# Relative-position attention with a binarised MLP: feed-forward jobs, normalisation steps and VectorE evacuations moved to other steps of a written-out order

## What is computed

```python
xn = layernorm(x)
x  = x + attn(xn) + ffn(xn)
# attn, 16 heads of 8 features: a second layernorm with gain and bias, then
content = einsum('bihd,bjhd->bhij', q + u_bias, k)
pos     = relative_shift(einsum('bihd,jhd->bhij', q + v_bias, p))
attn    = softmax((content + pos) * scale) @ v ;  attn = attn @ Wo + bo
# ffn: h = [xn, -xn], then three layers with weights of +1 or -1, 512, 512 and 128 wide
h = relu(s0 * h @ w0) * 2 ;  h = relu(s1 * h @ w1) * 2 ;  h = s2 * h @ w2
```

## Time and profile before

| | |
|---|---|
| median of 3 runs | 1533.58 us (1532.46 to 1533.88) |
| the profiled execution's own time | 1533.58 us |
| its span | 1531.8 us |
| granted TensorE clock, mean | 0.987 |
| TensorE (matmul) busy | 1488.4 us, 97% |
| VectorE busy | 1337.4 us, 87% |
| ScalarE busy | 1238.8 us, 81% |
| GpSimd busy | 717.8 us, 47% |
| DRAM traffic | 550.4 MB, 359 GB/s |
| load of a batch's x, issue to landing | 9.1 us, median of 16 |

### The profile page before, as it was taken

One profiled execution on the slowest core, in us unless ns is written; L12 is line 12 of the kernel. 1 busy time (PEld: TensorE's weight loads), 2 busy tenths in 40 slices (PEclk: granted clock), 3 DMA queues, 4 the chain that ended last, 5 costly groups with the idle time before them and its releaser, 6 DMA issues.

```text
span 1531.8 us, 41221 instructions
## 1 busy us (share of the span) xinstructions
PE 1488.4 (97%) x16040; PEld 981.4 (64%) x16040; DVE 1337.4 (87%) x3483; ACT 1238.8 (81%) x1368; POOL 717.8 (47%) x725
## 2 busy tenths in 40 slices
PE   6899999999999999999999999999999999999997
PEld 2466666666666666666666666666666666666664
DVE  4698989889898998989889898998989889898985
ACT  5688889888888888879888888888889888888873
POOL 5655636354563635537354463635536354533300
PEclk8799999999999999999999999999999999999998
DMA  3999999999999999999999999999999999999991
GB/s 132 331 373 363 374 381 368 385 352 396 367 372 387 348 393 362 359 387 361 386 358 387 367 367 393 352 388 367 377 383 360 388 363 386 362 384 368 369 412 65
DMA packets 80435, 550.40 MB, mean 359 GB/s; under 512 B 9329, under 2 KB 10097, under 8 KB 14705
## 3 DMA queue, kind: packets, MB, share of 16 engines
q1 hardware_dynamic: 42944, 278.35, 48.7%
q10 hardware_dynamic: 37296, 269.41, 46.9%
HBM read 274.57 MB, written 273.15 MB: 358 GB/s over the span
## 4 chain that ended last, share of the span: by engine, by line
PE 76%; DVE 13%; ACT 4%; DMA 3%; issue 3%; ACTq 0%; POOL 0%; DVEq 0%
PE ps_pt L694 27%; PE ps_av L708 13%; PE ps_job L635 12%; PE ps_pos L675 11%; DVE sc_sb L571 6%; DVE sc_sb L579 5%; PE ps_job L596 3%; PE ps_job L599 3%; DMA sc_sb<-shift 2%; PE ps_con L685 2%; ACT pt_sb L457 2%; PE ps_job L605 1%; ACT z_t L413 1%; PE ps_job L610 1%; PE ps_job L614 1%
## 5 line engine op out<-in xcount | busy, mean ns | idle before, releaser
L571 DVE CUSTOM_DVE_ANT_0 sc_sb<-ps_con,sc_sb 128x512 f32<-128x512 f32 x1024 | 664.2, 684 | 151.8 <-PE ps_con L685 143.8
L447 ACT COPY pos_sb<-ps_pos 128x1024 f32<-128x1024 f32 x510 | 519.0, 1018 | 139.8 <-PE ps_pos L675 135.3
L579 DVE TENSOR_SCALAR sc_sb<-sc_sb,nmax 128x512 f32<-128x512 f32 x1024 | 602.8, 620 | 0.1
L457 ACT ACTIVATE pt_sb<-ps_pt 128x1024 f32<-128x1024 f32 x512 | 524.8, 1025 | 59.0 <-PE ps_pt L694 57.0
L694 PE MATMUL ps_pt<-c_sb,sc_sb 128*128 128x128 f32 x4096 | 558.9, 280 | 7.9 <-ACT pt_sb L457 5.4
L694 PEld LDWEIGHTS ps_pt<-c_sb,sc_sb 128*128 128x128 f32 x4096 | 438.5, 141 | 134.9 <-issue 90.8
L708 PE MATMUL ps_av<-pt_sb,v_sb 128*9 128x128 f32 x8192 | 320.0, 274 | 1.3 <-issue 0.7
L685 PE MATMUL ps_con<-k_stack,q_stack 26*128 26x512 f32 x1024 | 301.3, 496 | 7.0 <-DVE nmax L571 1.9
L708 PEld LDWEIGHTS ps_av<-pt_sb,v_sb 128*9 128x9 f32 x8192 | 173.0, 90 | 196.5 <-issue 191.5
L675 PE MATMUL ps_pos<-p_stack,q_stack 26*128 26x512 f32 x1024 | 266.2, 500 | 6.7 <-ACT pos_sb L447 4.5
L351 POOL CAST h<-act_sb 128x512 fp32r<-128x512 f32 x128 | 78.6, 614 | 405.7 <-ACT act_sb L423 405.0
(11 more groups left out here) (88 smaller groups left out, 939.8 us busy)
## 6 DMA issues: line engine op xcount, KB each, us to landing
shift<-pos_sb SPq DMA_DIRECT2D x256, 1026.0 KB, 9.4
sc_sb<-shift ACTq DMA_DIRECT2D x256, 1024.0 KB, 10.6
x_sb<-in_x SPq DMA_DIRECT2D x16, 256.0 KB, 9.1
out<-x_sb SPq DMA_DIRECT2D x16, 256.0 KB, 11.2
stack_w_sb<-in_stack_w SPq DMA_DIRECT2D x1, 512.0 KB, 5.3
c_sb<-in_consts ACTq DMA_DIRECT2D x1, 422.0 KB, 3.3
o_t<-in_wp ACTq DMA_DIRECT2D x1, 256.0 KB, 5.9
heads<-in_pe_t ACTq DMA_DIRECT2D x1, 256.0 KB, 6.9
```

The lines of the kernel that those rows point to most:

```text
L447: act.copy(to, ps_pos[:, :, :]).then_inc(s_pe, 1)
L457: act.activation(pt_sb[:, 2 * i:2 * i + 2, :], ps_pt[:, :, :], ACT.Exp, scale=-1.0) \
L571: dve.tensor_tensor_reduce(sc_sb[:, m % N_SC, t, :], ps_con[:, k, :], sc_sb[:, m % N_SC, t, :], -SCALE, 3.4e38, ALU.add, ALU.min, nmax[:, ...
L579: dve.tensor_scalar(sc_sb[:, m % N_SC, t, :], sc_sb[:, m % N_SC, t, :], nmax[:, m % N_SC, t:t + 1], None, ALU.subtract).then_inc(s_sub, 1)
```

## The change

Three things move. (1) The tables: `L1 1` from half 6 to 5, `L0 0`, `L0 1` and `L0 2` of the next batch from halves 13, 14 and 19 to 18, 19 and 21, and `L0 3` from 32 (half 0 of the next batch) to 29. (2) `slot_of`: the statistics from slot 8 to 6 (half 16 to 12), `scales` and the first `norm` from slot 9 to 7 (half 18 to 14), the second `norm` from slot 11 to 10 (half 22 to 20). (3) On VectorE the copy of `ps_av` moves from the start of the half after to the end of the half itself, ahead of that half's jobs and statistics, and the jobs move from between the two subtractions to behind both and behind the copy.

```diff
         FIRST_NEXT = (... 
-                      (25, "V", 0), (27, "KG", 0), (32, "L0", 3))
+                      (25, "V", 0), (27, "KG", 0), (29, "L0", 3))
-        THIS = ((1, "QG", 1), (2, "L1", 0), (3, "KG", 1), (6, "L1", 1), (7, "QG", 2), (8, "L1", 2), (9, "KG", 2),
+        THIS = ((1, "QG", 1), (2, "L1", 0), (3, "KG", 1), (5, "L1", 1), (7, "QG", 2), (8, "L1", 2), (9, "KG", 2),
                 (10, "L1", 3), (15, "QG", 3), (16, "KG", 3), (28, "TO", 0), (30, "L2", 0, 2))
-        NEXT = ((11, "T1", 0), (13, "L0", 0), (14, "L0", 1), (17, "TZ", 0), (19, "L0", 2), (23, "QG", 0),
-                (25, "V", 0), (27, "KG", 0), (32, "L0", 3))
+        NEXT = ((11, "T1", 0), (17, "TZ", 0), (18, "L0", 0), (19, "L0", 1), (21, "L0", 2), (23, "QG", 0),
+                (25, "V", 0), (27, "KG", 0), (29, "L0", 3))
...
-            return [b if 0 <= b < B and slot == k else None for k in (8, 9, 11)]
+            return [b if 0 <= b < B and slot == k else None for k in (6, 7, 10)]
...
-                o, i = half_of(h - 1, VALUES_H)
-                if i == 1 and o % 4 == 3:
-                    ... wait for the values, copy ps_av to o_sb
                 todo = blocks(h, 2 * CONTENT_LAG)
...
-                if not todo:
-                    for j in taken(h):
-                        take_job(*j)
                 for k, (m, t) in enumerate(todo):
                     ... subtraction k
-                    if k == 0:
-                        for j in taken(h):
-                            take_job(*j)
+                o, i = half_of(h, VALUES_H)
+                if i == 1 and o % 4 == 3:
+                    ... wait for the values, copy ps_av to o_sb
+                for j in taken(h):
+                    take_job(*j)
```

More of the change, by code:

```diff
@@ L580, in _ @@
                                       nmax[:, m % N_SC, t:t + 1], None, ALU.subtract).then_inc(s_sub, 1)
-                    if k == 0:
-                        for j in taken(h):
-                            take_job(*j)
+                o, i = half_of(h, VALUES_H)
+                if i == 1 and o % 4 == 3:
+                    dve.wait_ge(s_av, 2 * (o + 1))
+                    k = o // GROUP
+                    if k >= 2:
+                        dve.wait_ge(s_job, job("TO", (k - 2) // GROUPS, (k - 2) % GROUPS))
+                    dve.tensor_copy(o_sb[:, k % 2, :, :], ps_av[:, :, :]).then_inc(s_oev, 1)
+                for j in taken(h):
+                    take_job(*j)
                 stat, _, _ = slot_of(h // 2)
```

## The result

The changed kernel takes 1549.3 us (median of 4 runs, 1546.02 to 1550.31), the kernel before beside it 1533.02 (1529.44 to 1533.88): ratio 1.0107, 95% interval 1.0085 to 1.013. It is slower by 16.3 us, where the prediction said 6.3; the time lies 0.3 us outside the range. The profiled execution took 1549.7 us with a span of 1547.9, so the two profiled executions differ by 16.1 us in both.

What follows compares the result with a forecast made beforehand. TensorE and VectorE run equally fast, coupled through waits, with TensorE idle some 3.8 of 91.6 us a batch. Terms +15.0, -1.2, -1.8 and -5.7 sum to +6.3 on 1533.6: 1540 us, 8-in-10 range 1530 to 1549.

Steps and rivals of the forecast that it cites:

- The statistics in half 12: Half 14: TensorE stalls 1.8 us waiting for VectorE, since empty halves hide nothing; halves 13 to 15 take 0.71 longer.
- Halves 18 to 22: Turn 19 comes 0.72 us late, L0 0 costing nothing inside an existing stall; turn 22 comes 1.15 late.
- The tie in half 20: Half 20: GpSimd beats VectorE by 0.16 us; rival, VectorE first: turn 22 0.38 earlier, 1535 us, no-change chance 0.20.
- L0 3 to 29: It goes into half 30's gap and half 0 becomes empty: a gain of 0.12 us per batch.
- L1 1 to 5: It takes up half 6's content wait of 0.73 us: a gain of 0.38 per batch after charges.
- The order on VectorE: Copy costs nothing; later jobs delay TY, KG and L0 3, with KG pushing turn 30 by 0.11 us.
- The norm steps: Norm beside VectorE's subtractions: costed at nothing, with 0.1 us per half as the other bound.
- The rival that norm holds up subtractions: Halves 14 and 15: norm holds a subtraction 0.45 us in each, giving 1552 us; chance 0.05.
- The first iteration: Half 12 lies where VectorE idles and half 17's 1.18 us goes: -1.2 us, once.
- DMA as the bound: Whole kernel: the DMA engines set the pace, so 1533.6 us; part of the no-change case, chance 0.20.
- ScalarE as the bound in halves 17 to 21: Its backlog doesn't clear, so one more evacuation (0.57 us) per batch lies on the path: 1547 us; chance 0.10.
- Lag absorbed: Half 14: the statistics cost TensorE nothing, 13 batches are 1.78 us better, giving 1517 us; chance 0.20.

Runs made afterwards that it cites:

- slots_only: Kernel before with only the new slots (statistics to half 12, both norm steps moved), old tables and VectorE order: 1553.9 us, ratio 1.016.
- stats_only: Kernel before with the statistics alone moved to slot 6 (half 12), norm steps in their old slots: 1554.25 us, ratio 1.0157.
- after_stats5: Changed kernel with the statistics one slot earlier, in slot 5 (half 10), all else as changed: 1526.9 us, ratio 0.9976.
- tables_only: Kernel before with only the new job tables, old slots and VectorE order: 1520.45 us, ratio 0.9936.
- tables_slots: Kernel before with the new tables and slots, VectorE's old order: 1542.83 us, ratio 1.0077.
- norm2_early: Changed kernel with statistics and first norm back in slots 8 and 9, second norm kept in slot 10: 1541.07 us, ratio 1.0061.
- order_only: Kernel before with only VectorE's new order (copy of ps_av in its own half, jobs behind both subtractions): 1539.1 us, ratio 1.0066.
- tables_stats5: Kernel before with the new tables and the statistics in slot 5 (half 10), old norm slots and VectorE order: 1515.08 us, ratio 0.9897.
- after_l13: Changed kernel with L0 0 put back in half 13: 1549.9 us, ratio 1.0125.

## Why the prediction was right in direction and short in size

**What failed.** The cause (the statistics stall half 14, because nothing covers them) and its price of 1.8 us were right. The sum was not: it gave +6.3 us, and +16.3 was measured. Two of its terms per batch were too small or too favourable: halves 12 to 22 at 1.15, measured 1.48, mostly since the emptied half 14 was counted at 2.01 and takes 2.27; and L1 1 to half 5 at a gain of 0.38, measured 0.22, since under the new order it waits 0.26 for TO, where 0.11 was charged. Two terms outside the batch were wrong as well: the first iteration, forecast at -1.2 and measured at +1.37, and TensorE's clock, which the sum does not have and which takes 3.4 us in three batches.

**The statistics in half 12: right.** Forecast: turn 14 at 795.28, which is 6.25 us behind turn 12 (791.05 - 2.45 + 0.43); measured 711.19 - 704.93 = 6.26. slots_only and stats_only show the same lateness without the rest of the change, and after_stats5 removes it, as the reason (empty halves hide nothing, eight products do) asks. The wait in the kernel after is 3.81 - 2.01 = 1.80 us, as forecast. It is what makes the change slower: with the statistics in half 10 instead (after_stats5) the same kernel is a little faster than before, ratio 0.9976.

**Halves 13 to 15: a term left out.** I let half 14, now empty, take 2.01 us, though I had the 2.24 of an empty half and used it for halves 0 and 6. Turn 14 to turn 15 took 2.27, with ScalarE's exp in between, as shown above. From half 15 to 19 the kernel was 0.98 late instead of 0.72: +0.26.

**Halves 18 to 22: right.** Turn 19 came 725.10 - 718.78 = 6.32 us behind half 17's positions (forecast 6.33), with L0 0 waiting 0.75 for `z_t` (0.6). The tie in half 20 went as forecast: in the kernel after GpSimd's operation began ahead of VectorE's pair, and L0 2 waited 0.46 for TO (0.2). VectorE, then GpSimd:

```profile
729.43 1.38 DVE L569 TENSOR_SCALAR sc_sb<-sc_sb,nmax 128x512 f32<-128x512 f32 x2
```

```profile
728.84 1.28 POOL L352 TENSOR_TENSOR h<-act_sb,h 128x512 fp32r<-128x512 f32 x1
```

Turn 22 is +1.48 instead of +1.15; of the 0.33, 0.26 is half 14's.

**L0 3 to 29: right in size.** From turn 22 (+1.48) to turn 1 (+1.38) the batch gains 0.10: 0.15 lost at turn 28, 0.05 back by turn 0, 0.20 gained at turn 1. Forecast: 0.12 net.

**L1 1 to 5: mis-sized.** Forecast 0.38, measured 0.22. With the old order it is 0.50 (tables_only, and tables_slots too), with the new one 0.20 to 0.22 in four kernels, so the order takes more than half of it: TO's evacuation stands behind both subtractions and L1 1 waits 0.26 for it, where I had charged 0.11.

**The order on VectorE: "nothing" was wrong.** I had looked only at the jobs that wait behind a job. What counts in half 20 is what runs while GpSimd holds VectorE: a job that reads PSUM fits into that time, and the new order takes this away. Alone it costs 0.6 us a batch; with the new slots, where other waits cover part, 0.2 to 0.25. It also made half 25 liable to a collision that the old order, with V between the subtractions, did not show (tables_only: TensorE never waits for V in the steady state).

**The norm steps: right.** stats_only and slots_only agree within 0.4 us. The rival that norm holds up subtractions gave 1552, close to what came, but not by its reason: no pair of subtractions in halves 13 and 14 of the kernel after takes more than 0.89 us. norm2_early adds that a norm step can cost indirectly, by what it delays on GpSimd.

**The first iteration: wrong sign.** I forecast -1.2; it was +1.37. In the kernel after L1 2's products take 3.06 us of loads from 59.41 on, at half the clock; before, 1.70 us from 60.93, at the full one. Ten of the twelve other kernels show less than the full clock in the same place, 60 to 64 us (all but order_only and tables_stats5). What decides it I can't say: with an equal wait ahead (1.63 us) tables_only fell to half the clock and tables_stats5 did not.

**The clock: not in the prediction at all**, 3.4 us in three batches, and -1.9 at the end.

**The other rivals.** VectorE losing or winning the tie, DMA as the bound, and ScalarE as the bound in halves 17 to 21 are refuted by the turns above; for loads VectorE waited only 4.5 us, in six waits. "Lag absorbed" needed a stall under 1.3 us in half 14; it was 1.80.

Of the miss of 16.1 - 6.3 = 9.8 us, 3.4 are half 14's loop (13 x 0.26), 2.1 L1 1 (13 x 0.16), 3.4 the clock and 2.6 the first iteration, 11.5 together. Against them stand the loads (-2.35) and the stretch behind the last TO (-1.9), and +1.6 in the last two iterations and +1.0 spread over the batches go the same way as the miss. The -1.9 goes with the clock and the +1.6 with waits for loads (see the table of the whole 16.1 us). What makes the loads late in one execution, and what decides the clock, I did not find out.

## What to carry to other kernels

Put side work of VectorE where the engine that sets the pace has jobs of its own in the same step and the next, not ahead of steps that have been emptied: in the kernel after the same 1.18 us of statistics led to 1.8 us of waiting from half 12, and to none beyond TO's old 0.43 from half 10, where L1 3 stands, with T1 in half 11. When jobs are moved, recompute every half that becomes empty with the pace of the loop that then binds it, and put VectorE operations that read PSUM into the time in which GpSimd holds up its SBUF operations (here worth 0.5 us in half 20). Take apart a change of several moves: here the tables alone gain 0.64%, and the order alone loses 0.66% and the slots alone 1.6%.

## What the hardware showed that I had not expected

**The clock falls behind a short wait, in some batches only.** In the kernel after all 13 batches have a TensorE wait of 1.43 us by these rows (1.00 + 0.43) in half 14; three of them, at 246, 618 and 990 us, are followed by about 4 us at 0.54 to 0.60 of the clock. They lie 372 us apart, which is four batches. tables_slots has three as well, at 151, 707 and 1263 us, evenly spaced too, by six batches. It has the same empty half 13 and waits of 1.01 + 0.43. In slots_only, stats_only and after_l13 turn 14 is as late, but a job in half 13 leaves waits of 0.38 to 0.54 + 0.43 us, and there is no fall. So in half 14 the falls go with the longer wait, in all five kernels that have these statistics in half 12; that the wait is what causes them is not shown, and why in only three of thirteen batches, I can't say. A wait of this length is not needed everywhere: norm2_early has a fall at 97 us behind waits of 0.73, 0.47 and 0.42 us. The Trainium skill, page "TensorE: Matmul & The Clock Gate", section "Part 1: The HAM clock gate", says that half the clock is the state at rest and that activity of the array lifts it; that fits the order of the rows, wait first and fall after it, but the section's account of idle gaps does not tell which of thirteen equal waits will be followed by a fall.

**A GpSimd operation can get in between two VectorE operations of one pair.** In slots_only the pair took 1.90 us, with GpSimd starting 0.25 us into it. The Trainium skill, page "SBUF — State Buffer", section "Who interferes with whom", says that whoever issues first has the shared ports for the whole instruction; the rows agree for tensor_tensor, one instruction at a time. They do not for the tensor_scalar of norm, beside which a pair of subtractions took 0.89 us in the kernel after (0.88 alone).
